# A decoder layer in fp32: the gate's logits as eight more columns of the cross attention's products, its choice and counts in one step

## What is computed

```python
x = layernorm(x + self_attention(x, Wq, Wk, Wv))                 # 16 heads of 16, one shared k and v
x = layernorm(x + cross_attention(x, ctx, ctx, mask, W1, b1, W2, b2))   # ctx [32, 120, 256], v is ctx itself
x = layernorm(x + ffn(x, Wg, W1, b1, Wo, bo))

def ffn(x, Wg, W1, b1, Wo, bo):                                  # 8 experts, top 2
    gate_scores = softmax(x @ Wg.T)
    topk_val, topk_idx = top_k(gate_scores, 2)
    topk_val = topk_val / (topk_val.sum(-1) + 1e-9)
    comb = (one_hot(topk_idx, 8) * topk_val[..., None]).sum(-2)
    out = 0
    for e in range(8):
        a, b = split(x @ W1[e].T + b1[e], 2)
        out += ((a * sigmoid(b)) @ Wo.T + bo) * comb[..., e:e+1]
    return out
```

## Time and profile before

| | us |
|---|---|
| median of 3 runs | 1431.65 (1428.14 to 1438.48) |
| profiled execution, its own time | 1429.97 |
| its span | 1428.1 |
| TensorE, VectorE, ScalarE, POOL busy | 1272.3, 1136.6, 742.4, 635.3 |
| TensorE's mean granted clock | 0.972 |

### The profile page before, as it was taken

One profiled execution on the slowest core, in us unless ns is written; L12 is line 12 of the kernel. 1 busy time (PEld: TensorE's weight loads), 2 busy tenths in 40 slices (PEclk: granted clock), 3 DMA queues, 4 the chain that ended last, 5 costly groups with the idle time before them and its releaser, 6 DMA issues. The chain is left out here.

```text
span 1428.1 us, 29996 instructions
## 1 busy us (share of the span) xinstructions
PE 1272.3 (89%) x7734; PEld 898.8 (63%) x7735; DVE 1136.6 (80%) x3121; ACT 742.4 (52%) x1716; POOL 635.3 (44%) x978
## 2 busy tenths in 40 slices
PE   6888899999899999999998559999999999968886
PEld 4443555556555555555553347888888888858786
DVE  0356788888888888888887778888888888859998
ACT  1225677777777777777777512222223332214444
POOL 3001244544454445445435343333333333348886
PEclk9999999999999999999999669999999999989999
DMA  7435475565674765665742854433343433379995
GB/s 165 99 74 87 84 120 116 117 128 124 121 132 114 131 120 119 129 125 112 132 96 77 332 181 135 133 128 131 132 134 134 134 129 129 133 270 330 334 341 186
DMA packets 171744, 212.39 MB, mean 149 GB/s; under 512 B 20032, under 2 KB 142912, under 8 KB 167424
## 3 DMA queue, kind: packets, MB, share of 16 engines
q1 hardware_dynamic: 147792, 144.32, 43.2%
q0 software_dynamic: 17488, 55.02, 10.3%
q10 hardware_dynamic: 6368, 11.89, 2.4%
HBM read 125.76 MB, written 85.71 MB: 148 GB/s over the span
## 5 line engine op out<-in xcount | busy, mean ns | idle before, releaser
L981 DVE TENSOR_REDUCE negmax<-psS 128x2 f32<-128x512 f32 x512 | 349.2, 686 | 99.6 <-PE psS L677 82.5
L820 ACT ACTIVATE probs<-psT 128x512 f32<-128x512 f32 x512 | 303.3, 598 | 168.8 <-PE psT L687 160.4
L1425 ACT ACTIVATE sig<-hb 128x512 f32<-128x512 f32 x135 | 85.4, 632 | 287.2 <-DVE hb L1501 280.1
L677 PE MATMUL psS<-kstack,qstack 96*128 96x256 bf16 x1024 | 195.0, 272 | 36.0 <-DVE kstack L1079 12.7
L687 PE MATMUL psT<-qstack,kstack 99*128 99x512 bf16 x512 | 193.7, 380 | 4.6 <-ACT probs L820 4.5
L1307 POOL DMA_INDIRECT g_rows<-g,slot x135 | 134.7, 998 | 70.0 <-issue 66.5
L677 PEld LDWEIGHTS psS<-kstack,qstack 96*128 96x128 bf16 x1024 | 92.3, 104 | 93.1 <-DVE negmax L981 34.6
L430 POOL DMA_INDIRECT lists<-x,slots x128 | 130.9, 1022 | 33.1 <-issue 30.2
L570 PE MATMUL psO<-probs,vaug 128*32 128x512 f32 x1024 | 137.2, 608 | 0.4 <-ACT probs L820 0.4
L1512 DVE SCALAR_TENSOR_TENSOR g<-g,xe,sig 128x512 f32<-128x512 f32 x135 | 101.4, 751 | 26.3 <-DVE g L1508 17.0
L1344 PE MATMUL psHb<-w_hi,xet_hi 128*128 x270 | 117.8, 436 | 0.0
(11 more groups left out here) (207 smaller groups left out, 2929.2 us busy)
## 6 DMA issues: line engine op xcount, KB each, us to landing
rows<-g_rows SPq DMA_DIRECT2D x32, 1024.0 KB, 8.1
qstack<-q_parts SPq DMA_DIRECT2D x192, 128.0 KB
xe<-lists SPq DMA_DIRECT2D x135, 133.0 KB, 2.1
q_parts<-qpart SPq DMA_DIRECT2D x32, 384.0 KB
sums<-x SPq DMA_DIRECT2D x32, 264.0 KB
x2in<-sums SPq DMA_DIRECT2D x32, 264.0 KB, 4.7
xt<-in_x_t SPq DMA_DIRECT2D x32, 256.0 KB
xres<-in_x SPq DMA_DIRECT2D x32, 256.0 KB
```

The source lines that it names most:

```text
L677: last = mm(psS[:, u % 2, hh * S:(hh + 1) * S], qstack[0:KROWS, b1.s4, 2 * hp + hh, c * P:(c + 1) * P], kstack[0:KROWS, b1.s4, :], start=T ...
L820: nc.scalar.activation(probs[:, u % PT, :], psT[:, u % 2, :], ACT.Exp, scale=SELF_SCALE).then_inc(sm["exp_done"], 1)
L981: v.tensor_reduce(negmax[:, b1.s2, 2 * hp:2 * hp + 2, c], psS[:, u % 2, :].rearrange("p (h k) -> p h k", h=2), AX.X, ALU.max, negate=True) ...
```

## The change

The gate's logits are no longer computed from x2. The norm of y2 is (y2 - mean) / std, and with gate weights from which the mean over the width is taken (wgc), the product of x2 with the gate is rstd times the product of y2 with wgc. y2 is the sum of x1 and the cross contexts, so its raw logits are the sum of two products that ride on others: keymap has eight more columns per batch (wgc), so the cross scores (L607, now 128 columns) also give x1's part; and ctxv has eight more columns (the context times wgc, two new products from a new load ctxt, placed behind the transposes of cprob at unit 9), so the contexts (L656, now 264 columns) give theirs. x1 and y2 are 264 wide. The second half of the contexts goes to psB.

Gone are the transposes of x2, x2t, the gate products and the copy of the logits. New are the copy of x1's raw part (unit 4), the product gneg = uneg * rstd2 on POOL, one load per step on SP, the products for wgc, and in the setup three operations on VectorE in front of cvec and two products on TensorE. The exponentials take rstd2 as their scale.

The choice moves forward in step n+6: maxima at units 0 and 1, indices at 2, topf at 4, hot at 5, hotsum at 6, the gate exponentials at unit 6 (from 11), the count products at unit 7 (from 15), place and base at 7, chosen at 8, gden at 9, 11 and 13, weights and slots at 15. There are 38 steps instead of 39.

Core of the diff:

```diff
-        for n in range(B + 7):
+        for n in range(B + 6):
...
+                sp.dma_start(ctxt[:, b.s2], io["context_t"][:, b.n * SC:(b.n + 1) * SC].rearrange("(c p) k -> p c k", p=P)
+                             ).then_inc(sm[f"ctxt_loaded{b.s2}"], 16)
...
+            wait(pool, "rstd2_ready", 4 * b.n + 2)
+            pool.tensor_tensor(gneg[:, b.s2], uneg[:, b.s2], rstd2[:, b.s2], ALU.mult).then_inc(sm["rstd2_ready"], 1)
...
+            for k in range(DC):
+                mm(psT[:, 0, DC:DC + E], ones[:, :], wg[:, k, :], start=k == 0, stop=k == DC - 1)
...
-        bank_b = {"q_projected": ("q_rest", 0, 1, 1), "x2_transposed": ("x2t_copied", 6, 1, 1),
-                  "gate_scored": ("gate_link", 6, 7, 1), "cprob_transposed": ("cprobt_copied", 5, 1, 1),
-                  "kv_projected": ("k_rest", 0, 1, 1), "counted": ("slot_link", 6, 3, 1)}
+        bank_b = {"q_projected": ("q_rest", 0, 1, 1), "counted": ("slot_link", 6, 3, 1),
+                  "cprob_transposed": ("cprobt_copied", 5, 1, 1), "kv_projected": ("k_rest", 0, 1, 1),
+                  "cross_out": ("y2_ready", 5, 1, 1)}
...
-                            last = mm(psA[:, c * SC:(c + 1) * SC], x1t[:, b5.s2, k, c * P:(c + 1) * P],
-                                      keymap[:, k, bass.ds(b5.n * SC, SC)], start=k == 0, stop=k == DC - 1)
+                            last = mm(psA[:, c * (SC + E):(c + 1) * (SC + E)], x1t[:, b5.s2, k, c * P:(c + 1) * P],
+                                      keymap[:, k, b5.n, :], start=k == 0, stop=k == DC - 1)
...
+                    wait(pe, f"ctxt_loaded{b5.s2}", 16 * b5.half + 16)
+                    for k in range(DC):
+                        last = mm(psB[0:SC, S:S + E], ctxt[:, b5.s2, k, :], wgc[:, k, :],
+                                  start=k == 0, stop=k == DC - 1)
...
-                        last = mm(psA[:, c * D:(c + 1) * D], cprob_t[:, b5.s2, c * P:(c + 1) * P], ctxv[:, b5.s2, :],
+                        last = mm((psA, psB)[c][:, 0:D + E], cprob_t[:, b5.s2, c * P:(c + 1) * P], ctxv[:, b5.s2, :],
...
+            v.scalar_tensor_tensor(wgc[:, :, :], psT[:, 0, DC:DC + E].unsqueeze(1).to_broadcast([P, DC, E]), -1.0 / D,
+                                   wg[:, :, :], ALU.mult, ALU.add)
+            for k in range(DC):
+                v.scalar_tensor_tensor(keymap[:, k, :, SC:SC + E],
+                                       psT[:, 0, DC:DC + E].unsqueeze(1).to_broadcast([P, B, E]), -1.0 / D,
+                                       wg[:, k, :].unsqueeze(1).to_broadcast([P, B, E]), ALU.mult, ALU.add)
...
+            if u == 6:
+                link(3)
+                wait(dve, "counted", done(b.back(2)))
+                v.tensor_tensor(hotsum[:, b.s2], hot[:, b.s2, :, 0, :], hot[:, b.s2, :, 1, :], ALU.add
+                                ).then_inc(sm["hot_ready"], 1)
```

More of the change, by code:

```diff
@@ L316, in load_xt, with store_x2 @@
                              ).then_inc(sm[f"xt_loaded{b.s2}"], 16)
+        def store_x2(b):
+            wait(sp, "comb_ready", done(b))
+            rows = dram["sum"].rearrange("(b s) d -> b s d", s=S)[bass.ds(b.n, 1)]
+            sp.dma_start(rows.rearrange("o (c p) d -> p (o c) d", p=P), x2[:, b.s2, :, 0:D + E]
+                         ).then_inc(sm[f"x2_stored{b.s2}"], 16)
         def step(t):
@@ L321, in step @@
                 load_setup()
[L322 to L327, removed]
+            if active(t.back(7)) and t.n <= B + 1:
+                store_x2(t.back(7))
             b = t.back(3)
@@ L356, in step @@
                 load_experts(t)
+            if active(t.back(6)) and draining(t):
+                store_x2(t.back(6))
         pipeline(sp, step)
@@ L437, in step @@
             if active(b6) and draining(t):
-                power(b6, vare2, rstd2, "rstd2_ready")
+                power(b6, vare2, rstd2, "rstd2_ready", 4)
             elif active(b6):
-                rstd(b6, "var2_ready", mv2, vare2, nmean2, rstd2, shift2, "rstd2_ready")
+                wait(pool, "gate_exp", done(b6.back(2)))
+                rstd(b6, "var2_ready", mv2, vare2, nmean2, rstd2, shift2, "rstd2_ready", per=4)
+                scale_max(b6)
             if active(t):
@@ L453, in step @@
                 expert_constants()
-            if active(b7):
-                if not active(t):
-                    wait(pool, "slots_ready", done(b7))
+            late = active(b7) and t.n <= B + 1
+            if late:
                 dispatch(b7, 0)
@@ L861, in stats @@
             for c in range(QC):
[L862 removed]
+                last = v.bn_stats(out[:, b.s2, c, :], y[:, b.s2, c, 0:D])
             last.then_inc(sm[name], 1)
@@ L941, in drain_slot @@
                 v.tensor_copy(x1t[:, b5.s2].rearrange("p c s -> p (c s)"), psA[:, :]).then_inc(sm["x1t_copied"], 1)
-            if active(b6) and u == 6:
-                wait(dve, "x2_transposed", done(b6))
-                wait(dve, "gate_scored", done(b6.back(2)))
-                v.tensor_copy(x2t[:, b6.s2].rearrange("p c s -> p (c s)"), psB[:, :]).then_inc(sm["x2t_copied"], 1)
             if active(b4):
@@ L973, in step @@
                     wait(dve, "stats2_ready", done(b6))
-                if u == 9 and active(b6):
-                    wait(dve, "gate_max", done(b6))
                 if u == 13 and active(b4) and not draining(t):
@@ L1100, in step @@
                 copy_keybias(g)
-            if active(b6):
-                gate(7)
-                wait(dve, "hot_ready", done(b6))
-                for c in range(QC):
-                    v.scalar_tensor_tensor(x2[:, b6.s2, c, D:D + E], gexp[:, b6.s2, c, :],
-                                                  gden[:, b6.s2, c:c + 1], hotsum[:, b6.s2, c, :], ALU.mult, ALU.mult)
-                v.tensor_copy(x2[:, b6.s2, :, D + E + 1], topf[:, b6.s2, :, 0]).then_inc(sm["comb_ready"], 1)
-                if not b6.fixed or b6.n >= 2:
-                    v.tensor_scalar(x2[:, b6.s2, :, D + E], x2[:, b6.s2, :, D + E], float(4 * S), None, ALU.add)
-                wait(dve, "counted", done(b6))
-                wait(dve, "slot_link", 3 * b6.n - 2)
-                count = psB[:, 0:3 * E].rearrange("p (c e) -> p c e", e=E)
-                now, then = base[:, b6.s2, :], base[:, 1 - b6.s2, :]
-                v.tensor_tensor(place[:, b6.s2], count[:, 0:QC, :], now.unsqueeze(1).to_broadcast([P, QC, E]), ALU.add)
-                v.tensor_tensor(then, count[:, QC, :], now, ALU.add).then_inc(sm["slot_link"], 1)
         pipeline(dve, step)
```

263 lines of the change are left out of this document (135 added, 128 removed).

## The result

| | before | after |
|---|---|---|
| median of 4 runs, us | 1429.89 | 1482.41 |
| lowest to highest | 1424.85 to 1438.48 | 1481.65 to 1488.75 |
| span of the profiled execution | 1428.1 | 1480.9 |
| TensorE's mean granted clock in it | 0.972 | 0.935 |

The kernel is slower by 3.7% (ratio 1.0367, 95% interval 1.0332 to 1.0403). The prediction said 1436, within 1% of before, and its range ended at 1449: it was wrong.

The account below looks back on a forecast made before the run. It took the step to hang on TensorE from unit 5 to 14, then on VectorE and ScalarE. 1429.97 + 10.4 (steps) - 7 (drain) + 1.8 (setup) = 1435.2, put at 1436 for the median; range 1414 to 1449.

Parts of the forecast that it names:

- The plain step, 22.2: Steady attention steps 6 to 31: each about 0.4 us longer than 21.82, in all 26 x 0.4 = +10.4 us.
- The two products in front of S(9), 0.41: Unit 9: two fp32 products of context and centred gate, on TensorE's own chain, add 0.41 us a step.
- Case C: Rival: the small products hide under another wait, the rest as forecast; 1425 us, chance 0.15.
- TensorE stands some 1.8 us there, and the whole relief ... is spent: +0.1.: Unit 7: the count waits for hotsum, using up TensorE's 2.3 us relief; S(7) at 504.9 against 504.83.
- The first view: Profile stretches of the attention stage, 400 to 600 us: TensorE busy 186 of 200 us at granted clock 1.00.
- The drain, -7: Last steps, where the chain is latency: removing the gate from it saves 7 us, between 9 and 4.
- now those transposes need no gate: Step 36 of the drain: the transposes of cprob go earlier, y2 of the last batch at 814.4, -4 us.
- -6.4: Step 37 of the drain: the gate needs y2 alone, so the table starts at 824 instead of 830.41.
- The setup, +1.8: Setup: three VectorE operations before cvec (0.95 us) and added TensorE records (0.85); +1.8, bounds 0 and +2.5.
- A: Rival, faster: TensorE's relief survives and the step falls to what the query ring allows; 1414 us, chance 0.2.
- B: Rival, slower: ScalarE's burst or place and base delay cprob's transposes, +0.9 a step; 1450 us, chance 0.2.
- The recorded sum: Whole kernel: 1429.97 + 10.4 - 7 + 1.8 = 1435.2 us; with the median 1.7 above, forecast 1436.

Follow-up runs that it names:

- e1: Kernel after with filler products whose result is written over, 6 ahead of unit 6's wait and 12 ahead of unit 7's hotsum wait; 1447.42 us.
- e8: e1 with the two products of the context and centred gate weights moved from unit 9 to unit 7, ahead of the hotsum wait; 1441.57 us.
- e5: Kernel after with hotsum moved behind cnegmax in unit 5 and POOL's indirect writes of the drain one step later; 1424.36 us.
- e6: e5 with the two products of the context and centred gate weights moved from unit 9 to unit 7, ahead of the count products; 1422.80 us.
- e11: Kernel before, with unit 7's gate products waiting for VectorE's maximum of unit 6 and three added VectorE copies; 1512.17 us.
- e2: Kernel after with POOL's indirect writes in the drain (steps 33 to 36) issued one step later, behind the second norm's power; 1471.73 us.
- e13: e6 plus 6 fillers in unit 6 and 8 ahead of S(0), with step 36's three W1 halves moved behind place and base; 1415.56 us.
- e3: Kernel before with one wait added: unit 7's gate products wait for VectorE's maximum of unit 6; 1451.99 us.
- e4: Kernel after with hotsum moved from behind the maximum of unit 6 to behind cnegmax in unit 5; 1437.30 us.
- e9: Kernel after with only the 6 filler products of unit 6; unit 7's wait for hotsum stays; 1448.12 us.

## Why the prediction was wrong, point by point

**The plain step, 22.2: right within 0.2.** It is 22.02, so 26 x 0.2 = +5 us instead of +10.4. The argument held: TensorE's relief is spent by waits for VectorE. hotsum starts 0.60 us behind the maximum of unit 6, as worked out; that maximum stands 9.58 us behind S(0), where 9.85 was put, and the difference carries to S(7) (10.54 against the 10.85 of "504.9"). TensorE stands 1.0 + 0.74 = 1.74 us, where "some 1.8 us there" was written, but in two places. The half at unit 6, for the reader of psA, was not seen: topf and the copy of the raw logits were counted for the maxima, and not for cscore, which releases psA.

**The two products in front of S(9), 0.41: right.** S(7) to S(9) grew by 0.41 us, and moving them gave 0.34 per step in both pairs (e1 and e8, e5 and e6). The row of L629 was the right measure. By the floor of 25 ns from start to start of the Trainium skill (TensorE: Matmul & The Clock Gate, "Back-to-back issue gap") it would have been 0.1; the same section says that its gap for a small product leaves the weight load out. Each of these products loads a new weight tile, and the rows say 0.1 us per record. Case C falls with it.

**The step that failed: "TensorE stands some 1.8 us there, and the whole relief ... is spent: +0.1."** This took standing as free. The runs show that it was not: the long steps at a granted clock of 0.50 cost 38.4 us, filling the idle time gives 35 back (e1), and lengthening it in the kernel before brings the same 38 (e11). The sum had no term for the clock. The first view read gave it as 1.00, and the forecast then put nearly 2 us of standing into each step. The trace of before even has such a fall, in step 4, which the prediction did not look at (timeline, and windows):

```profile
122.32 0.39 PE L677 MATMUL psS<-kstack,qstack 96*128 96x256 bf16 x2 [3.23 <-DMA qstack<-q_parts]
```

```profile
122.00:123.00 1.00, 0.68 (x7) 0.34 (x11) 0.25 (x1) 0.02 (x1) 0.00 (x0) 0.89 1.10 345
123.00:126.00 3.00, 3.00 (x13) 1.03 (x13) 1.05 (x2) 0.76 (x2) 0.00 (x0) 0.50 0.13 37
```

TensorE stands for late query parts, starts, and runs at 0.50 for some 3 us. The Trainium skill describes such a swing in another kernel (TensorE: Matmul & The Clock Gate, "A second HAM failure mode: psum-queue depth-cycling": a kernel whose TensorE idles briefly and often between groups of products swings between the two levels). The traces of after and e11 agree, with a fall in 15 and 17 of the 26 steps, here behind waits for VectorE.

**The drain, -7: wrong in sign, +9.3.** Three steps of the argument, each with its run. First, POOL's queue: the four indirect writes were moved past rstd, and the prediction counted them nowhere; e2 puts them back and gives 10.7 us. Second, "now those transposes need no gate" in step 36 (-4): they need psB, which the count products hold until place has read it, and place stands behind three halves of W1, where the copy of the logits stood before. The prediction named this bank's wait for the steady steps and dropped it here. Moved behind place, the halves give 2.7 us (e13), and they still bind there: ScalarE's roundings, which the prediction put next, hold the copy of cprob until 802.5, but the contexts are done before the halves are. Third, step 37: its -6.4 holds the -4 of step 36, so 2.4 were put for the last piece, y2 to the table. In after it takes 12.3 us against 12.06 before; with POOL's order mended 8.8, so 3.2 us came. Both mends together, and the two products at unit 7 (e13), bring the stretch from y2 of step 31 to the table to 90.4 us, 5.7 under before: most of the -7 was there to be had, but not in this order of the queues.

**The setup, +1.8: met by +2.0, which is luck as far as is known.** The thirteen traces with the new setup (after and twelve experiments) reach y2 of step 5 between 166.2 and 171.4 us, the three with the old one at 165.2 (before), 163.7 (e3) and 172.8 (e11). The first steps wait for query parts and have falls of the clock of their own, and what the setup costs is lost in that.

**The rivals.** A (1414) was refused on the ground that even a step without a gate gains at most 0.9 and that hotsum would be late. Its step of 21.4 is what e4 has, with hotsum early, so the room was judged rightly. Its total of 1414 is near e13's 1415.6, but by another sum (21.08 us for the plain step, 5.7 us in the drain). B (1450) named ScalarE's burst and place; neither wait appears in the steady steps. Slower came out, but from a cause that no rival named. The recorded sum itself is 0.9 us short: 1435.2 and the 1.7 of the median are 1436.9, which changes nothing here.

## What to carry to other kernels

When a change makes TensorE stand for another engine in the middle of a dense stretch, price the clock as well as the wait: look where the waits sum up within a step, and what the steps cost at half speed. An operation of 0.16 us that another engine waits for belongs in front of a long one, not behind it, and a short stall that cannot go may be filled with products that nobody reads. Every move past a queue (here POOL's writes past rstd, and place behind W1's halves) is followed on that queue up to the next one who waits for it.

## What was not expected of the hardware

Two waits that leave the clock alone when either is cut short cost 38 us together. Per step TensorE stood 0.74 + 1.0 us (after) or 0.9 + 1.4 us (e11) when the clock fell; it stood 0.3 + 1.0, 0.8 + 0.3, 0.7 + 0.4 and (in before's order) 0.9 + 0.6 us when it did not; single stands ahead of S(0) of 2.1 and 1.7 us (e6) and 3.2 us (before, step 4) also brought it down, and another one of 1.7 us (e6) did not. With the stand ahead of S(0) counted in, all of TensorE's idle time in the 26 steps comes to 2.4 us per step in after and e2 and 2.8 in e11, the kernels with falls in most steps, and to 2.0 in e3, 1.9 in e9 and less in the others. In after the fall comes in some steps and not in others that stand equally long, so the sum per step is not the whole of it, and what decides between the 22.0 and the 25.1 us steps stays open. The price of a fall is plainer: a step of 25.1 against 22.0, some 7 us at 0.50, in which VectorE and ScalarE wait for TensorE.
